# An attention and expert layer on one core: the value products of a slot go between its two heads, later jobs move back

## The reference, cut to what matters

```python
scores = jnp.einsum('bhqd,bhkd->bhqk', Q, K) * scale
attn = jax.nn.softmax(scores, axis=-1)
attended = jnp.einsum('bhqk,bhkd->bhqd', attn, V)
...
x = _layernorm(x + attended @ Wo + bo)
s = sigmoid(x @ router_w.T)            # 8 experts, the best 2 with ties by index
comb = gates of the two, 0 elsewhere
shared = (silu(x @ sw1) * (x @ sw3)) @ sw2
routed = sum over experts of comb * (gelu(x @ ew1[e]) @ ew2[e])
x = _layernorm(x + shared + routed)
```

## Time and profile before

| | |
|---|---|
| median of the runs shown | 232.91 us |
| profiled execution | 230.98 us |
| its span | 229.2 us |
| PE busy | 207.9 us (91%) |
| PE weight loads busy | 120.0 us (52%) |
| DVE busy | 157.3 us (69%) |
| ACT busy | 137.9 us (60%) |
| POOL busy | 107.5 us (47%) |
| mean granted clock of TensorE | 0.974 |

### The profile page before, as it was taken

How to read it: one execution, slowest core, us unless ns; L and a number is a source line. 1 busy time by engine, 2 the same in 40 slices (tenths; PEclk the granted TensorE clock), 3 DMA queues, 4 the chain that set the end, 5 groups by cost and what they waited for, 6 DMA issues and landing times.

```text
span 229.2 us, 4496 instructions
## 1 busy us (share of the span) xinstructions
PE 207.9 (91%) x1538; PEld 120.0 (52%) x1538; DVE 157.3 (69%) x333; ACT 137.9 (60%) x280; POOL 107.5 (47%) x208
## 2 busy tenths in 40 slices
PE   7998979989998989999899999899998999999970
PEld 7764555435564645546454554466664455645520
DVE  6688877849899899989994030664548655556654
ACT  2899464878877778778778877334341533534330
POOL 8787997023506379582965156144003802020203
PEclk9999955999999999999999999999999999999998
DMA  4391654384410000009000350000090010541011
GB/s 154 107 258 31 167 166 104 99 307 104 103 27 6 3 6 4 9 3 366 10 3 6 140 233 0 3 1 0 3 366 0 3 47 1 182 186 46 3 44 48
DMA packets 10422, 19.19 MB, mean 84 GB/s; under 512 B 1952, under 2 KB 7008, under 8 KB 9760
## 3 DMA queue, kind: packets, MB, share of 16 engines
q1 hardware_dynamic: 8976, 17.06, 22.7%
q10 hardware_dynamic: 1040, 1.05, 1.3%
q0 software_dynamic: 384, 0.79, 1.3%
HBM read 12.80 MB, written 1.11 MB: 61 GB/s over the span
## 4 chain that ended last, share of the span: by engine, by line
PE 68%; DVE 18%; ACT 7%; issue 4%; ACTq 1%; POOL 0%; POOLq 0%; DVEq 0%
PE ring L800 14%; PE pv_bank L826 10%; PE max_bank L960 9%; DVE top L672 8%; PE sum_bank L960 4%; PE ring L782 3%; PE ring L780 3%; PE ring L781 3%; ACT probs_mem L570 3%; PE max_bank L809 3%; PE pv_bank L834 2%; DVE hid L750 2%; PE misc_bank L882 1%; ACT xt L645 1%; PE misc_bank L780 1%
## 5 line engine op out<-in xcount | busy, mean ns | idle before, releaser
L672 DVE TENSOR_REDUCE top<-max_bank 128x2 f32<-128x512 f32 x128 | 81.0, 682 | 10.7 <-PE max_bank L809 10.4
L570 ACT ACTIVATE probs_mem<-ring 128x512 f32<-128x512 f32 x128 | 70.0, 596 | 19.4 <-PE ring L800 17.8
L800 PE MATMUL ring<-qstack,kstack 32*128 32x256 f32 x256 | 45.5, 336 | 6.4 <-ACT probs_mem L570 3.7
L809 PE MATMUL max_bank<-kstack,qstack 32*128 32x256 f32 x256 | 44.4, 338 | 1.1 <-DVE top L672 0.8
L800 PEld LDWEIGHTS ring<-qstack,kstack 32*128 32x128 f32 x256 | 29.3, 190 | 27.1 <-ACT probs_mem L570 16.1
L826 PE MATMUL pv_bank<-probs_mem,v 128*18 128x256 f32 x512 | 41.4, 397 | 0.4 <-ACT probs_mem L570 0.4
L750 DVE TENSOR_TENSOR hid<-xt,gates_mem 128x512 f32<-128x512 f32 x32 | 22.5, 703 | 24.0 <-ACT xt L645 24.0
L645 ACT ACTIVATE xt<-ring 128x512 f32<-128x512 f32 x32 | 19.1, 598 | 32.4 <-PE ring L782 32.4
L960 PE MATMUL max_bank<-hid,wf 128*128 128x512 f32 x60 | 32.0, 614 | 1.7 <-DVE hid L750 1.4
L809 PEld LDWEIGHTS max_bank<-kstack,qstack 32*128 32x128 f32 x256 | 28.3, 190 | 5.9 <-POOL kstack L475 1.8
L780 PE MATMUL ring<-yt_hi,wf_lo 128*128 128x512 f32 x40 | 31.3, 782 | 0.0
(11 more groups left out here) (191 smaller groups left out, 333.2 us busy)
## 6 DMA issues: line engine op xcount, KB each, us to landing
gates_mem<-gate_scratch SPq DMA_DIRECT2D x4, 2048.0 KB, 7.2
kstack<-gates_mem SPq DMA_DIRECT2D x36, 64.0 KB, 2.1
qstack<-gates_mem SPq DMA_DIRECT2D x24, 64.0 KB, 2.1
wf<-w_ffn_dram SPq DMA_DIRECT2D x1, 1408.0 KB, 6.3
xs<-x_dram SPq DMA_DIRECT2D x4, 256.0 KB, 5.4
xt<-x_t_dram SPq DMA_DIRECT2D x3, 256.0 KB, 4.4
qstack<-gates_mem POOLq DMA_DIRECT2D x12, 64.0 KB, 2.3
out_dram<-xs SPq DMA_DIRECT2D x3, 256.0 KB, 2.3
```

Of the source, the lines that this page charges most:

```text
L570: nc.scalar.activation(probs[:, i % 2, s_heads(s)[r], :], ring_of(("scores", 2 * s + r))[:, :], ACT.Exp, scale=SCALE).then_inc(probs_made, 1)
L672: dve.tensor_reduce(top[:, m_heads(m)[r], t, :], max_bank[(2 * m + r) % NMAX][:, :].rearrange("p (h k) -> p h k", h=2), AX.X, ALU.max).the ...
L800: ins = mm(ring_of(("scores", 2 * s + r))[:, kt * S:(kt + 1) * S], kstack[rows, t, k:k + P], qstack[rows, t, b * S:(b + 1) * S], start=Tru ...
L809: ins = mm(max_bank[(2 * m + r) % NMAX][:, qt * S:(qt + 1) * S], qstack[rows, t, q:q + P], kstack[rows, t, b * S:(b + 1) * S], start=True, ...
```

## The change

Three things change. `times_v` moves from behind the second half to between the halves: S0, products, S1, jobs. The jobs `wo`, `y` and `yT` of a batch come one slot later, `router` six slots later, and with it the routing, `combT` and `load gates` of groups 0 to 2; in the tail the routing of group 3 and the router of batch 7 come one slot later, `combT` 4 and 5 four, `load gates` 2 three, while `combT` 6 and 7 and `load gates` 3 stay. And `router` is cut in two jobs of three matmuls each, `router0` and `router`, one slot apart in attention and in the same slot in the tail; the bank belongs to both.

```diff
-        for kind, n in (("norm", 2), ("attT", 3), ("wo", 4), ("y", 5), ("yT", 8)):
+        for kind, n in (("norm", 2), ("attT", 3), ("wo", 5), ("y", 6), ("yT", 9)):
             put(first + n, (kind, b))
         if b < NB - 2:
-            put(first + 9, ("router", b))
+            put(first + 14, ("router0", b))
+            put(first + 15, ("router", b))
         if b % 2:
             for kind, n in route:
-                put(first + 9 + n, (kind, b // 2))
+                put(first + 15 + n, (kind, b // 2))
             if b // 2 < 2:
-                put(first + 22, ("combT", b - 1))
-                put(first + 23, ("combT", b))
-                put(first + 25, ("load gates", b // 2))
+                put(first + 28, ("combT", b - 1))
+                put(first + 29, ("combT", b))
+                put(first + 31, ("load gates", b // 2))
...
-    for n, job in ((2, ("norm", NB - 1)), (4, ("attT", NB - 1)), (5, ("wo", NB - 1)), (5, ("y", NB - 1)), (8, ("router", NB - 2)),
-                   (9, ("combT", 4)), (10, ("yT", NB - 1)), (10, ("combT", 5)), (11, ("router", NB - 1)), (12, ("load gates", 2)),
-                   (24, ("combT", NB - 2)), (25, ("combT", NB - 1)), (26, ("load gates", 3))):
+    for n, job in ((2, ("norm", NB - 1)), (4, ("attT", NB - 1)), (5, ("wo", NB - 1)), (5, ("y", NB - 1)), (8, ("router0", NB - 2)),
+                   (8, ("router", NB - 2)), (10, ("yT", NB - 1)), (12, ("router0", NB - 1)), (12, ("router", NB - 1)),
+                   (13, ("combT", 4)), (14, ("combT", 5)), (15, ("load gates", 2)), (24, ("combT", NB - 2)), (25, ("combT", NB - 1)), (26, ("load gates", 3))):
         put(NHALF + n, job)
     for kind, n in route:
-        put(NHALF + 11 + n, (kind, NG - 1))
+        put(NHALF + 12 + n, (kind, NG - 1))
...
                             scores(s, r, t)
                         if m is not None:
                             maxima(m, r, t)
-                for p in slot.pv:
-                    times_v(p)
+                    for p in slot.pv if r == 0 else ():
+                        times_v(p)
                 for kind, b in slot.jobs:
                     if kind in TAKER:
                         misc = misc_of((kind, b))
+                    if kind in TAKER and kind != "router":
                         wait_bank(pe, (kind, b))
+                    if kind == "router0":
+                        wait_bank(pe, ("router", b))
...
-                    if kind == "router":
-                        pe.wait_ge(rw_split, 1)
-                        wait_taken(pe, ("yT", b))
-                        for t in range(QT):
-                            tok = slice((QT * b + t) * P, (QT * b + t + 1) * P)
-                            ins = three(misc[:, t * NE:(t + 1) * NE], yt_hi[:, tok], yt_lo[:, tok],
-                                        rw_parts[:, 0, :], rw_parts[:, 1, :], True, True)
-                        ins.then_inc(misc_made, 1)
+                    if kind in ("router0", "router"):
+
+                        misc, t = misc_of(("router", b)), int(kind == "router")
+                        if kind == "router0":
+                            pe.wait_ge(rw_split, 1)
+                            wait_taken(pe, ("yT", b))
+                        tok = slice((QT * b + t) * P, (QT * b + t + 1) * P)
+                        ins = three(misc[:, t * NE:(t + 1) * NE], yt_hi[:, tok], yt_lo[:, tok],
+                                    rw_parts[:, 0, :], rw_parts[:, 1, :], True, True)
+                        if t:
+                            ins.then_inc(misc_made, 1)
```

## The result

The kernel after takes 289.4 us (median of 6 executions, 278.7 to 294.2), the kernel before 233.2 on the same chip (6 executions, 230.9 to 233.6): 1.204 times as long, interval 1.192 to 1.216. The forecast was 240.9 us, its range 235 to 248; the sign was right, and of the loss of 56 us I had foreseen 8. The ratio leaves out executions far above the fastest of their kernel, and the profiled one (294.18 us) is among those; its six executions differ in TensorE's mean granted clock, 0.749 at 294.2 us and 0.810 at 278.7, and that is the subject of what follows.

What follows compares the result with a forecast made beforehand. TensorE and DVE both looked full; PE waited 2.5 us a block, less slack than the change asks for. Terms 5.3 + 0.3 + 2.0 + 0.4 = +8.0 on 232.91 gave 240.9 us, range 235 to 248.

Steps and rivals of the forecast that it cites:

- the sum over slots 16 to 63: Attention slots 16 to 63: 85.2 us of TensorE work against 79.93, +5.3, called a floor even if every wait vanishes.
- a half there (0.75 us): Slots 2 to 4, clock at 1.2 GHz: a half takes 0.75 us; one stays exposed, +0.8.
- the clock might rise earlier: Early slots, part of the no-change rival: extra work falls into existing waits, 232.9 us within 1.2, chance 0.08.
- Halves 0.43 ahead of and behind products of 0.56: Sign in attention slots: one half starts 0.43 us ahead of the products, the other 0.56 behind their start.
- Blocks of 14.0 to 14.3: Sign in attention: eight-slot blocks last about 14.0 to 14.3 us from one yT to the next, 13.35 before.
- DVE's share near 0.88: Sign in attention blocks: DVE's busy share falls near 0.88, from 12.47 of 13.35 us before.
- Slots 2 to 15, +2.3 forecast: Early slots: +2.0 us for slots 2 to 13 and +0.3 for slots 14 and 15, which have no job.
- Slots 52 to 63 +2 us: Sign at the end of attention: the 12 slots without maxima get longer by some 2 us.
- 1 us of idle before group 3's first combT: Tail: group 3's den goes one slot later, combT stays, so PE waits for comb, +1.0 us.
- No idle before unit 14's second product: Tail: new bank rotation removes 0.93 us of idle; the next unit waits about 0.4 for DVE, net -0.6.
- Tail: Behind attention: +1.0 us of waiting for comb and -0.6 at unit 14, net +0.4.
- the third rival: Attention blocks: DVE and ACT hand on half of the 2.5 us waits, +7.7 over six blocks, 248.6 us, chance 0.15.

Runs made afterwards that it cites:

- experiment 4: Kernel after plus full-width matmuls as filling behind the value products in three of four slots: with three 296.3 us, with one 283.8 us.
- experiments 1 and 6: Kernel before: 1, with only the value products moved between the halves, 293.2 us; 6, with three full-width matmuls added in three of four slots, 243.9 us.
- experiment 5: Kernel after plus twelve-matmul bursts at the head of slots 24, 32, 40, 48, 56: on 128 rows 260.8 us, on 32 rows 308.9 us.
- the jobs alone: Kernel after with the value products put back behind both halves, leaving moved jobs and the router in two pieces: 236.9 us, ratio 1.024.
- experiment 3's second order: Kernel after with each slot as first half, jobs of the slot before, value products, second half: 263.3 us.

## Why the prediction was wrong

The step that failed is the sum over slots 16 to 63: "That is 85.2 us of TensorE work in program order ... It is a floor". It takes every duration from rows at 2.4 GHz and holds that clock for the new order. I had read the fives of the earlier trace rows as something of slots 2 to 4, priced a half there (0.75 us), and asked only whether the clock might rise earlier. No term, no rival and no bound had a fall; measured, the fall costs 50.8 us. The rival could have been worked out from rows of before: halves of 0.75 instead of 0.43 and the rest at twice its time make 8 x (0.75 + 1.12 + 0.75) + 5.8 for the jobs (twice 2.9), some 26.7 us a block (an estimate), against 24.22 measured.

The other steps, by the list of what would show them:
- Halves 0.43 ahead of and behind products of 0.56: right, as far as the clock held.
- Blocks of 14.0 to 14.3: 14.73. TensorE's work was right (14.21 busy); 0.5 us a block is waiting, for exp and for ACT's copy of the products (0.2 each in that block), which I had left out of the sum. Over six blocks +7.9 (an estimate from the block of slots 12 to 20, not from one yT to the next: the second yT lies in the low stretch), not +5.3.
- DVE's share near 0.88: 0.86 (12.66 of 14.73).
- Slots 2 to 15, +2.3 forecast: +4.0 measured (products of slot 16 at 64.53, before at 60.51).
- Slots 52 to 63 +2 us: can't be told, they lie in the low stretch.
- 1 us of idle before group 3's first combT, released by comb: 0.94, at 256.03. No idle before unit 14's second product: none at 235.34; the next one waits 0.66 for DVE (0.4 forecast). Tail +0.5, with 2.4 us of the lower clock in it, against +0.4.

With the clock held, then, the kernel after comes to 230.98 + 4.0 + 7.9 + 0.5 = 243.4 by the profiled execution, an estimate from its own rows; 239.0 was forecast. The one execution of experiment 4 with three matmuls that held the clock, 265.7 us, less 46 x 3 x 0.17 of filling, gives 242.2, an estimate too. So the change would lose at 2.4 GHz as well. That part of the mechanism was right and some 4.4 us too small; the missing 50.8 are the clock. That the third rival ("the waits stay", 248.6) lies nearer to the result is no merit: its blocks over 15 us were to show PE idle for ACT or DVE, and PE is busy 24.22 of 24.22.

The rule of the Trainium skill that the prediction weighed ("Perfetto Trace Analysis", section Identifying the Most-Contended Engine: TensorE's headroom by the busy share of weight loads, beside the share of peak that the matmuls reach) did not help at either level: the share is 54% (7.92 of 14.73) at the upper and 52% (12.56 of 24.22) at the lower, where TensorE alone sets the pace.

The Trainium skill, "TensorE: Matmul & The Clock Gate", Part 1, section What's actually happening, has the lower level as the default and says that activity releases the throttle. The return behind the first units agrees. Read as busy time it does not: 129.71 of 129.71 us busy at 0.50. In the bursts the clock came back behind matmuls on 128 rows and not behind as many on 32.

Shown is, then, that parting the halves brings the long fall (experiments 1 and 6), and that dense full-width matmuls end it where as many on one strip do not (experiment 5). That the clock falls because fewer strips work at a time is argued from these, not shown by itself. What stays open: why executions of one kernel differ by up to 41 us (one matmul of filling, 270.6 to 311.5), why three matmuls of filling held the clock in one execution of four only, and what ended falls with no unit and no added matmul near: that of the jobs alone at 142.5, 4 us ahead of the first unit (146.4), and one of experiment 3's second order at 95.5. Halves together are no full safeguard either: three of 22 executions of the kernel before beside the experiments took 241 us at a mean clock of 0.915, where the profiled one has 0.974.

## What to carry to other kernels

Before the order of a busy TensorE is changed, look at what runs side by side in its array: matmuls that overlap on different strips are cheap in time and may also be what keeps the clock up, and in this kernel parting them cost 64% of a block by the clock (24.22 against 14.73) on top of the 10% that the change itself cost (14.73 against 13.41). Price every TensorE-bound stretch a second time by rows at the lower clock, as a rival of its own. And read the clock line ahead of the busy line: at the lower level PE looks simply full.

## What the runs showed of the hardware

- The granted clock fell to 1.2 GHz with TensorE 92% busy and stayed there for 129.71 us without an idle moment; at 97% busy with wider use it stayed at 2.4 GHz.
- The value products keep all 128 rows at work in every slot, and so do the jobs; they did not hold the clock in the kernel after, though they take about half of TensorE's time there (eight slots with 2 x 0.43 of halves are 6.9 us of 14.73). But the profile prints the products' weights as 128*18, and four start side by side (104.40 to 104.42 in the kernel before): all rows, not all columns of the array.
- Twelve matmuls of 128*128 in a burst brought the clock back (low for 3.4 us in two falls, 260.8 us in all); twelve of 32*128 at the same places did not (low for 133 us, 308.9 us).
